# Four chained attention layers on one core: the head of the next batch made inside the last layer of the present one

## What is computed

```python
def reference(x, ...):                       # x: (8, 256, 32, 32) float32
    # L0: attention with 8 heads of 32, over N = 1024 tokens
    tokens = x.reshape(B, C, N).transpose(0, 2, 1)
    q, k, v = split((tokens @ w_proj + b_proj).reshape(B, N, 8, 96))
    attn = softmax(einsum('bihd,bjhd->bijh', q, k) * 32 ** -0.5, axis=2)
    x = (einsum('bijh,bjhd->bihd', attn, v) @ w_out + b_out + tokens).T
    # L1: group norm, one-head attention over 256 channels, residual
    # L2: instance norm, one-head attention (unscaled), residual
    # L3: kt = conv1x1(x, w_qk); xp = avg_pool(x); qt, vt = conv1x1(xp, ...)
    #     pi = softmax(mix_weight . mean(kt))
    #     z = w_out . ((softmax(kt2) @ vt2 * pi) summed / sqrt(32) @ q)
    mu, var = z.mean(axis=(0, 2, 3)), z.var(axis=(0, 2, 3))      # all batches
    return (z - mu) * rsqrt(var + 1e-5) * bn_weight + bn_bias + x
```

## Time and profile before

| what | value |
| --- | --- |
| median of 3 runs | 3090.85 us (3090.58 to 3091.7) |
| the profiled execution | 3092.63 us |
| its span, first to last instruction | 3090.9 us |
| PE busy / DVE / ACT / POOL | 87% / 66% / 41% / 21% |
| mean granted TensorE clock | 0.937 of full speed |
| from one batch to the next | about 375.5 us |

### The profile page before, as it was taken

One profiled execution on the slowest core, in us unless ns is written; L12 is line 12 of the kernel. 1 busy time (PEld: TensorE's weight loads), 2 busy tenths in 40 slices (PEclk: granted clock), 3 DMA queues, 4 the chain that ended last, 5 costly groups with the idle time before them and its releaser, 6 DMA issues.

```text
span 3090.9 us, 44860 instructions
## 1 busy us (share of the span) xinstructions
PE 2674.5 (87%) x15742; PEld 1889.2 (61%) x15742; DVE 2051.6 (66%) x2355; ACT 1279.2 (41%) x1860; POOL 635.7 (21%) x405
## 2 busy tenths in 40 slices
PE   6889979899798897988879888899888899888993
PEld 4457755577556775567755677457764477645772
DVE  4666667666676676666667566765677666766666
ACT  2553326433264333643336333463334533255334
POOL 0520116102160022500225002340024200252011
PEclk8999989999899998999999999999999999999996
DMA  6100050000500005000040001400022000410016
GB/s 150 32 25 1 1 130 2 25 1 14 117 1 25 1 14 117 2 24 1 21 110 1 24 1 36 95 12 14 1 66 66 25 1 1 95 37 25 1 55 245
DMA packets 46397, 124.71 MB, mean 40 GB/s; under 512 B 9792, under 2 KB 21312, under 8 KB 42560
## 3 DMA queue, kind: packets, MB, share of 16 engines
q1 hardware_dynamic: 46144, 121.41, 14.4%
HBM read 43.01 MB, written 23.86 MB: 22 GB/s over the span
## 4 chain that ended last, share of the span: by engine, by line
PE 74%; DVE 8%; issue 5%; ACT 5%; SPq 4%; DMA 3%; DVEq 0%; ACTq 0%
PE tile L1356 24%; PE pv L1356 10%; PE pv L1474 8%; PE tile L1436 7%; PE tile L1464 6%; PE tile L1623 4%; PE tile L1498 4%; SPq L522 3%; DMA stack<-qk_r 2%; PE pv L1464 2%; PE tile L1645 2%; PE tile L1753 1%; PE tile L1672 1%; PE tile L1523 1%; PE tile L1506 1%
## 5 line engine op out<-in xcount | busy, mean ns | idle before, releaser
L965 DVE TENSOR_REDUCE small<-tile 128x1 f32<-128x1024 f32 x512 | 599.1, 1218 | 169.8 <-PE tile L1436 169.8
L744 ACT ACTIVATE p<-tile 128x512 f32<-128x512 f32 (+1 forms) x640 | 410.2, 688 | 234.0 <-PE tile L1464 233.9
L1436 PE MATMUL tile<-stack 96*128 96x512 f32 x1024 | 348.8, 437 | 83.0 <-ACT stack L752 49.1
L1356 PE MATMUL tile<-qk_r 128*128 128x512 f32 x1536 | 377.9, 395 | 0.0
L653 POOL TENSOR_TENSOR row_sum<-act 128x256 f32<-128x256 f32 x32 | 42.1, 1334 | 1501.4 <-DVE act L1191 1501.4
L623 POOL TENSOR_TENSOR acc<-acc,p 128x1024 f32<-128x1024 f32 x144 | 339.4, 2385 | 0.0
L1436 PEld LDWEIGHTS tile<-stack 96*128 96x128 f32 x1024 | 177.8, 196 | 255.5 <-issue 118.1
L1356 PEld LDWEIGHTS tile<-qk_r 128*128 128x128 f32 x1536 | 287.1, 188 | 66.4 <-issue 7.7
L1196 DVE TENSOR_TENSOR pl<-p,ph 128x1024 fp32r<-128x1024 f32 x128 | 158.2, 1236 | 238.0 <-ACT p L838 238.0
L1464 PE MATMUL tile<-stack 112*128 112x512 f32 x768 | 271.2, 421 | 16.1 <-DVE rec L1013 9.2
L1474 PE MATMUL pv<-p,v 128*32 128x512 f32 x2048 | 271.8, 604 | 1.4 <-ACT p L744 1.4
(11 more groups left out here) (285 smaller groups left out, 4546.6 us busy)
## 6 DMA issues: line engine op xcount, KB each, us to landing
stack<-qk_r SPq DMA_DIRECT2D x192, 256.0 KB, 5.0
x_in<-in_x_dram SPq DMA_DIRECT2D x9, 1024.0 KB, 7.6
act<-in_x_dram SPq DMA_DIRECT2D x8, 1024.0 KB, 8.0
x_scratch<-act SPq DMA_DIRECT2D x7, 1024.0 KB, 3.9
z_scratch<-zbuf SPq DMA_DIRECT2D x7, 1024.0 KB, 5.3
stack<-ones SPq DMA_DIRECT2D x8, 512.0 KB, 7.6
w3f<-w3f_scratch SPq DMA_DIRECT2D x8, 512.0 KB, 3.3
fin_rest<-z_scratch SPq DMA_DIRECT2D x3, 1024.0 KB, 12.7
```

The costliest lines, as they stand in the source:

```text
L744: sc.activation(p0[:, jt % DEPTH, pair, first:first + len(heads) * HALF], tile_wait(b, "st0", *u, jt, k), ACT.Exp, scale=float(D) ** -0.5) ...
L965: ve.tensor_reduce(maxima[:, h * NT + it:h * NT + it + 1], t[:], X, ALU.max).then_inc(vector_done, vector.one("max0", g, h, it))
L1356: ins = mm(out, lhs[a][kt_], rhs[c][kt_], start=first and kt_ == 0 and m == 0, stop=last and kt_ == n - 1 and m == 2)
L1436: ins = mm(o[:, s], stack[0:IMAX, 0, g, h, it * P:(it + 1) * P], stack[0:IMAX, 1, g, h, s], start=True, stop=True)
```

## The change

The head is taken out of the front of the loop body and woven into the tail of the body, for the next batch. Each engine's program is now a function `turn(b, first, last)` that is laid down three times: once with the head of batch 0 alone, once as the loop body (seven rounds: layers 0 to 3 of batch b with the head of batch b + 1), and once as batch 7 without a head. POOL's loop stays as it was. With that:

- `x_hi` and `x_lo` are made in halves, and no longer for the first batch in the setup, nor once too often in the last batch.
- In the tail, DVE makes both `windows` before `mt_in`; `qv`, `mt` and `g` use the `pv` PSUM tile, and the three rotating tiles are left to the rest.
- `qk_r` and `stack` are laid out by head group, so that group 0 of `stack` can be filled while layer 3 still uses the memory under group 1. `smt` is split into `side` rather than `qk_r`; `gh` and `gl` share memory with `raw`; `z` is kept in `act` (after its store to `x3_scratch`), and `zbuf` is gone (`zlast` in the last batch).
- SP issues `key_ones` and the 12 DMAs of each group apart. ACT waits for group 0's before the first exponential and for group 1's before key tile 2, not for all before `max_cols`. `act` of the next batch is loaded after the store of `z` has ended.
- The final loads go to other places with other waits: six batches are issued before the last `z`, one after it.

```diff
 def tensor_steps():
-    s = [("qk0", t, g) for g in range(NG) for t in range(2)]
-    for k in range(G * HT):
-        s += [("v0", k // 3 - 1)] if k in (3, 6, 9, 12) else []
-        s += [("s0", *rows_of(UNITS[0], k))]
-    s += [("m0", 0, 0)]
+    s = []
...
-    s += [("kt", 0), ("kt", 1), ("qv",), ("mt",), ("g",), ("smt", 0), ("smt", 1), ("z", 0), ("z", 1)]
-    return s
+    s += [("kt", 0), ("kt", 1), ("qv",), ("qk0", 0, 0), ("qk0", 1, 0), ("mt",), ("qk0", 0, 1), ("g",), ("qk0", 1, 1)]
+    for k in range(G * HT):
+        s += {0: [("smt", 0), ("v0", 0)], 2: [("smt", 1)], 4: [("v0", 1)], 6: [("z", 0)], 8: [("z", 1)],
+              10: [("v0", 2)], 12: [("v0", 3)]}.get(k, [])
+        s += [("s0", *rows_of(UNITS[0], k))]
+    return s + [("m0", *UNITS[0])]
...
 def scalar_steps():
-    s += [("kt_exp", 0), ("x_hi", 0), ("x_hi", 1), ("kt_exp", 1), ("mix_exp",), ("smt_hi", 0), ("g_hi", 0), ("g_hi", 1)]
-    s += [("smt_hi", 1), ("z_kept", 0), ("z_kept", 1)]
-    return s
+    s += [("x_hi", 0, ct) for ct in range(CT)] + [("kt_exp", 0)] + [("x_hi", 1, ct) for ct in range(CT)] + [("kt_exp", 1)]
+    s += [("qk0_hi", 0, 0), ("qk0_hi", 1, 0), ("qk0_hi", 0, 1), ("mix_exp",), ("qk0_hi", 1, 1)]
+    s += [("g_hi", 0), ("g_hi", 1), ("smt_hi", 0), ("v0_kept", 0), ("smt_hi", 1), ("v0_kept", 1), ("z_kept", 0)]
+    s += [("z_kept", 1), ("v0_kept", 2), ("v0_kept", 3)]
+    return s + [("max_cols", *UNITS[0], t) for t in range(HT)]
...
 def vector_steps():
+    s += [("win_max", 0), ("kt_sub", 0)] + [("x_lo", 0, ct) for ct in range(CT)]
+    s += [("stat", 3, 1, ct) for ct in range(CT)] + [("mv", 3, 0), ("mv", 3, 1), ("win_max", 1), ("kt_sub", 1)]
+    s += [("x_lo", 1, ct) for ct in range(CT)] + [("qv_in",), ("win_sum", 0), ("win_rec", 0)]
+    s += [("win_sum", 1), ("win_rec", 1), ("sm", 1), ("qk0_lo", 0, 0), ("qk0_lo", 1, 0), ("mt_in",), ("kbar",)]
+    s += [("qk0_lo", 0, 1)] + [("mix", k) for k in range(4)] + [("mix_sum",), ("mix_rec",), ("mix_pi",), ("qk0_lo", 1, 1)]
+    s += [("smt_lo", 0), ("g_lo", 0), ("g_lo", 1)]
+    for k in range(G * HT):
+        s += {2: [("smt_lo", 1)], 9: [("z_stat", 0, 0), ("z_stat", 0, 1)],
+              12: [("z_stat", 1, 0), ("z_stat", 1, 1)]}.get(k, [])
+        s += [("max0", *rows_of(UNITS[0], k))]
+    s += [(n, *UNITS[0]) for n in ("neg_hi", "neg_copy", "neg_lo")]
+    return s + [("max_rows", *UNITS[0], h) for h in range(G // 2)]
...
+        if kind in ("qv", "mt", "g"):
+            home[n] = (SLOTS, None)
+            continue
...
+            def turn(n, first=False, last=False):
+                batch = n - 1
+                if not first:
+                    sp.wait_ge(tensor_done, tensor.at(batch, "pv0", *UNITS[-1], NT - 1))
+                    sp.dma_start(w3f[:], w3f_dram).then_inc(w3_back, 16)
+                    sp.dma_start(wo3[:], wo3_dram).then_inc(w3_back, 16)
                 if last:
                     return
...
+                key_ones(0)
+                sp.wait_ge(vector_done, vector.at(n, "qk0_lo", 1, 0))
+                stack_parts(0)
+                if not first:
+                    sp.wait_ge(tensor_done, tensor.at(batch, "smt", 1))
+                key_ones(1)
+                sp.wait_ge(vector_done, vector.at(n, "qk0_lo", 1, 1))
+                stack_parts(1)
+                if not first:
+                    sp.wait_ge(vector_done, vector.at(batch, "z_stat", CT - 1, 1))
+                    sp.dma_start(z_dram[n], act[:]).then_inc(z_stored, 16)
+                    sp.wait_ge(z_stored, 16 * n)
+                sp.dma_start(act[:], x_v[n]).then_inc(act_loaded, 16)
+            turn(0, first=True)
+            with sp.Fori(1, B) as n:
+                turn(n)
+            turn(B, last=True)
...
                 if b == 0:
-                    sp.wait_ge(tensor_done, tensor.at(B - 1, "v", 2, 1))
-                elif b == 1:
                     sp.wait_ge(tensor_done, tensor.at(B - 1, "st", 2, NT - 1))
                 elif b == 2:
-                    sp.wait_ge(vector_done, vector.at(B - 1, "x_lo", CT - 1))
+                    sp.wait_ge(tensor_done, tensor.at(B - 1, "pv", 2, NT - 1))
                 elif b == 3:
+                    sp.wait_ge(tensor_done, tensor.at(B - 1, "kt", 1))
+                elif b == 4:
+                    sp.wait_ge(tensor_done, tensor.at(B - 1, "smt", 1))
+                elif b == 6:
                     sp.wait_ge(tensor_done, tensor.at(B - 1, "z", CT - 1))
...
-                for s in stacked[0] + stacked[1]:
-                    act_e.wait_ge(s, 48 * b + 48)
...
+                        if not former and jt in (0, DEPTH // 2):
+                            for arrived in stacked[jt // (DEPTH // 2)]:
+                                act_e.wait_ge(arrived, 48 * b + 48)
```

More of the change, by code:

```diff
@@ L223, in pool_steps, with of_head @@
     return s
+def of_head(name):
+    kind, unit = name[0], name[1:3]
+    if kind in ("s0", "max0"):
+        return name[1] == 0 and name[3] < HT
+    if kind in ("m0", "neg_hi", "neg_copy", "neg_lo", "max_rows", "max_cols"):
+        return unit == UNITS[0]
+    return kind in ("qk0", "v0", "qk0_hi", "v0_kept", "qk0_lo", "x_hi", "x_lo")
 class Steps:
@@ new lines, in turn @@
+                head, body = not last, not first
+                for k in range(2):
+                    if head:
+                        x_hi(k)
+                    if body:
+                        kt_exp(k)
+                if head:
+                    qk0_hi(0, 0)
+                    qk0_hi(1, 0)
+                    qk0_hi(0, 1)
+                if body:
+                    act_e.wait_ge(vector_done, vector.at(b, "mix", 3))
+                    sc.activation(mix_e, logits, ACT.Exp).then_inc(scalar_done, scalar.one("mix_exp"))
@@ new lines, in turn @@
+                if body:
+                    smt_hi(1)
+                if head:
+                    v0_kept(1)
+                if body:
+                    z_kept(0)
+                    z_kept(1)
+                if head:
+                    v0_kept(2)
+                    v0_kept(3)
+                    max_cols(b + 1, *UNITS[0])
+                assert not scalar.made
+            turn(-1, first=True)
+            with act_e.Fori(0, B - 1) as b:
+                turn(b)
+            turn(B - 1, last=True)
@@ L935, in _ @@
             STT(b3_parts[:], tmp[:, 0:C], ident[:, D:D + 1], acc[:, 0:C], ALU.mult, ALU.add).then_inc(setup_vector, 1)
[L936 to L943 removed]
+            ve.memset(small[:], 0.0).then_inc(setup_vector, 1)
@@ L1310, in _ @@
                                     ).then_inc(vector_done, vector.one("z_stat", ct, k))
-                assert not vector.todo
+                head, body = not last, not first
+                if body:
+                    feat_lo(3, 1)
+                    window_maxima(0)
+                if head:
+                    x_lo(0)
+                if body:
+                    statistics(3, 1)
+                    aggregate(3)
+                    window_maxima(1)
+                if head:
+                    x_lo(1)
@@ new lines, in turn @@
+                if head:
+                    qk0_lo(1, 1)
+                if body:
+                    smt_lo(0)
+                    g_lo(0)
+                    g_lo(1)
+                for k in range(G * HT):
+                    if body and k == 2:
+                        smt_lo(1)
+                    if body and k in (9, 12):
+                        z_stat((k - 9) // 3)
+                    if head:
+                        max0(*rows_of(UNITS[0], k))
+                if head:
+                    max_rows(*UNITS[0])
@@ L1314, in _ @@
+                assert not vector.made
+            turn(-1, first=True)
+            with dve.Fori(0, B - 1) as b:
+                turn(b)
+            turn(B - 1, last=True)
             chain = 0
```

578 lines of the change are left out of this document (293 added, 285 removed).

## The result

The changed kernel takes **3008.8 us** (median of 4 runs, 3006.0 to 3010.1) against 3091.3 (3090.6 to 3094.3) beside it: a ratio of 0.973, 95% interval 0.9713 to 0.9747. The forecast was 3002, with 2985 to 3028 as its range. The profiled execution took 3008.4 with a span of 3006.7, 84.2 us less than before; the forecast was 88.6 less.

What follows compares the result with a forecast made beforehand. The bound was the chain of waits around a batch's end, tail then next head, which neither PE nor DVE fills. Terms 60.6 + 12.6 + 4.5 + 10.9 = 88.6 us gained, from 3090.9 to 3002; range 2985 to 3028.

Steps and rivals of the forecast that it cites:

- last batch's tail: Last batch, up to the last `z`: `mt_in` stands behind both window sums, so `z` ends 1 us later.
- The woven stretch: From `feat_lo` to `m0`: DVE is the limit, with 10.1 us of waits; `m0` 8.05 us earlier in each boundary.
- The stacks are no longer late: At a boundary: group 1's stack DMAs land by 819; ACT asks for them at key tile 2, behind 830.
- I take 4.7 us after m0: At the loop's turn: units start 4.7 us after `m0`, between branch rows of 3.72 and 5.3 us.
- the branch costs nothing: Rival, chance 0.07, at the loop's turn: 2.25 us instead of 4.7, six times 2.45, 14.7 us; time 2987.
- Disturbed fetches: Rival, chance 0.10, at the turn: three code fetches disturb one another and the load of `act`; 21 us, time 3023.
- Lower clock in part: Rival, chance 0.12: PE at the lower clock in part of the woven stretch; 4 us a boundary, 28, time 3030.
- Slower: Rival, chance 0.03: PE at the lower clock for the whole woven stretch, being fed in small pieces; time 3230.
- not woven: Rival, chance 0.02: a wait holds DVE's `qk0_lo` behind the tail; only stack wait and end gain; time 3059.
- The first batch: First batch: gains only the wait for group 1's stacks, 6.8 - 2.25 = 4.5 us.
- `m0` is bound by the same maxima: First batch's head: `m0` is bound by the same maxima, so only the stack wait's 4.5 us is gained.
- The end: After the last `z`: one load pair left, then stores; ends at 3080, 10.9 us gained, 8 to 14.

Runs made afterwards that it cites:

- unwoven: pad64 with each turn's tail and next head one after the other again on all engines; 3047.4 us.
- act_late: Changed kernel with the load of `act` held back by one wait on SP until `pv0` of the first unit; 3006.6 us.
- branch_m0: pad64 with PE's loop turn moved from behind `m0` to right ahead of `m0`; 3009.4 us.
- branch_pe: Changed kernel with PE's loop turn alone moved from behind `m0` to behind layer 2's first value tile; 2985.7 us.
- tail_tiles: Kernel with PE's turn behind layer 2's first value tile and 32 padding instructions, plus two other PSUM tiles for `z(0)`, `z(1)` in the last tail; 2983.6 us.
- pad64: Changed kernel with 32 more instructions (long-met waits) in PE's setup, ahead of the loop; 2986.2 us.

## Why the prediction held, and where it was wrong

The time was inside the range, 7 us over the forecast, and the mechanism of its largest term, the weaving, was right. That the number came out so near is luck: `m0` came earlier than forecast by 17 us in all, the end gave 1 more, and the other four terms lost 23. (Another 2 us are that the forecast set time and span equal; the profiled execution took 1.7 more than its span.)

| term | forecast | measured |
|---|---|---|
| `m0` earlier, seven boundaries, each | 8.05 | 10.5 |
| units' start behind `m0`, six boundaries, each | 2.1 | 0.0 |
| the same, seventh | 4.55 | 3.8 |
| first batch | 4.5 | 0.5 |
| last batch's tail | -1.0 | -6.5 |
| behind the last `z` | 11.9 | 13.1 |

**The woven stretch.** Right in its mechanism and its bound: DVE sets it. The waits laid out by hand were 10.1 us and are 9.9; `feat_lo` to `m0` is 54.5 us (1119.11 to 1173.61) where 56.1 was forecast. What was too large is the floor: DVE's work from the end of `feat_lo` to the last `max_rows` (end 1175.9) is 56.8 - 9.9 = 46.9 us, not 47.9, and `m0` stands 2.3 us ahead of that end, not 1.9. In this boundary `m0` stands 9.65 us nearer to `feat_lo` than before; the table's 10.5 is a mean over the seven and has small gains outside the boundary in it. unwoven gives 9.1 for the order alone.

**"The stacks are no longer late"**: right. `max_cols` waits for `m0` (6.79), no wait of ACT for a stack is in the boundary.

**"I take 4.7 us after m0"**: the first `s0` comes 4.04 us behind, and the branch row of 3.72 that this rests on measured 3.55. The other row, DVE's 5.3, is 2.9 to 3.5 in the changed kernel. The step that failed is that it costed a branch as one stall. PE fetches a piece of 16 KB, and how much of that piece lies behind the target depends on where the loop head happens to stand; here it was some 15 instructions, and a second fetch followed at once, behind the load of `act`. That is 2.6 us a turn more, 15.5 in all. The first exponential stands 9.33 us behind `m0`, as before (9.32). In the seventh boundary, without a branch, `s0` follows `m0` by 2.73 us and not 2.25, and that of the kernel before was 6.55 there, not 6.8: hence 3.8 and not 4.55. The prediction did say that the load would be in flight, and read nothing from it but a bound.

**The price of a branch.** PE's branch that is not taken lasts 83 ns, the taken ones 3.3 to 7.6 us. The 108 ns of the Trainium skill (Advanced Engine Details and Errata, Control Flow Timing) come near the first alone. So the rival "the branch costs nothing" holds in the seventh boundary only, and the rows that the forecast went by were the better guide. The page that names the cause, Runtime: NRT & Kernel Launch in the Trainium skill (Instruction fetch mechanics), wasn't weighed in the prediction; it would have led to the question of where the loop head stands.

**The rivals.** *Disturbed fetches* was the nearest: not the three branches disturb one another, but a transfer's packets stand ahead of a fetch (act_late, unwoven, branch_m0). PE's branch lasts as long with those of DVE and ACT beside it (3.35 to 3.79 in the changed kernel) as without (3.32 to 3.91 in branch_pe). This rival had 3023 for 3.5 us a turn. *Lower clock in part*: not in the woven stretch (0.96), but in the stall it is 0.50, and in the two rounds without weaving 0.66 to 0.83. *Slower* and *not woven* didn't happen.

**The first batch.** The stack wait went, 4.1 us of the 4.5 forecast (`m0` to exp 9.26 to 5.19), but `m0` came 3.6 us later. The step failed in "`m0` is bound by the same maxima": the new order puts `v0`'s tiles later among them, and PE, at 0.66 and 0.83 of its clock, held DVE up. warm shows 2.0 of it as the clock's; unwoven, with the old order, has it all back (78.69).

**The end.** The window of 405 GB/s and the one pair left behind `z` are as forecast, and the loads have left the chain: it now goes through DVE's adds, the last of them starting at 3000.1. The last tail is the failed step: 1 us was given for `mt_in`, and 6.5 were lost, since the PSUM tiles were dealt out for a woven order. Without the head, `smt(1)`, `z(0)` and `z(1)` follow one another in the same tile. tail_tiles takes 3.9 us of it back. The prediction looked at the order of the last round, but not at its tiles.

## What to carry to other kernels

When a loop's turn is moved, ask three things of the new place: does the engine's sequencer run ahead there, or does the whole program start from it; how far behind the loop head does the next piece of 256 instructions begin; and what is in the DMA queues at that moment. A turn belongs where its engine waits for something else and the queues are empty. And an order woven for the middle of a loop should be read once more for the first and the last round, with its tiles and its clock.

## What the runs showed of the hardware

- A taken loop branch on PE lasts 3.3 to 3.9 us where the DMA queues are quiet (before, branch_pe) or little used (the changed kernel, pad64), 4.3 to 5.1 among the small stack transfers (unwoven, DMA share 0.97), 5.1 to 7.6 behind these and a 1 MB store (branch_m0); one not taken lasts 83 ns.
- PE resumes 2.3 to 2.8 us after the 16 KB packet of its code is seen in the queue (3.0 once, in act_late). If the next piece begins some 15 instructions on, the two stalls follow each other: 2.6 us more. With the loop head 32 instructions further it is gone, with 256 it is back.
- 32 instructions that do nothing made this kernel 0.75% faster. Two kernels whose code differs in length can differ by this alone, whatever the edit was for.
- Making the first head's `s0` products twice (warm) kept PE's granted clock at 1.00 and 0.97, where it was 0.66 and 0.83, and brought the first `m0` 2 us earlier.
- Kernels that do the same work in the same order can differ by about a microsecond a batch by the clock alone: the same projections of layer 1 had 0.72 in pad64 and 0.55 in branch_pe.
